# Recurrence operations of the two halves joined into one instruction each, router columns joined to the first up unit, two gated products given to VectorE

## The reference

```
q, k = l2norm(silu(h Wq)), l2norm(silu(h Wk));  v = silu(h Wv);  beta = sigmoid(h Wb)
u_t = beta_t * (v_t - S_{t-1}^T k_t)         # one state S (16 x 16) for each image and head
S_t = S_{t-1} + k_t u_t^T ;  o_t = S_t^T q_t # 256 tokens, one after the other
x1  = x + h + o Wo
n   = layernorm(x1);  p = softmax(n router_w), the two largest kept and normalised
y   = alpha * shared(n) + (1 - alpha) * sum_e p_e * ((silu(n Wg_e) * (n Wu_e)) Wd_e)
out = x1 + y ;  alpha = sigmoid(n sg_w + sg_b)
```

## Time and profile before

| | us |
|---|---|
| median of 3 runs (497.37 to 498.15) | 497.47 |
| the profiled execution | 497.98 |
| its span | 496.2 |
| VectorE busy in the span | 428.0 |
| TensorE busy | 425.9 |
| GpSimd busy | 414.0 |
| ScalarE busy | 349.7 |

### The profile page before, as it was taken

How to read it: one execution, slowest core, us unless ns; L and a number is a source line. 1 busy time by engine, 2 the same in 40 slices (tenths; PEclk the granted TensorE clock), 3 DMA queues, 4 the chain that set the end, 5 groups by cost and what they waited for, 6 DMA issues and landing times.

```text
span 496.2 us, 10722 instructions
## 1 busy us (share of the span) xinstructions
PE 425.9 (86%) x2464; PEld 391.3 (79%) x2464; DVE 428.0 (86%) x2546; ACT 349.7 (70%) x1039; POOL 414.0 (83%) x527
## 2 busy tenths in 40 slices
PE   0344276899999999999999999999999989899996
PEld 0233144789999989899898989898988979898996
DVE  2349989999999999999999999999999999997200
ACT  2795445686878787877778686878786848385763
POOL 5288699989899999999999898998999999896341
PEclk9855555999999999999999999999999999999999
DMA  7948373543323222323233332323222323200300
GB/s 203 223 100 159 94 180 100 111 103 111 79 68 88 72 78 74 92 65 102 68 84 87 81 89 78 89 72 83 80 83 74 83 78 86 81 28 0 114 2 16
DMA packets 44752, 44.12 MB, mean 89 GB/s; under 512 B 19920, under 2 KB 36496, under 8 KB 44688
## 3 DMA queue, kind: packets, MB, share of 16 engines
q1 hardware_dynamic: 40944, 40.87, 32.3%
q10 hardware_dynamic: 3744, 2.57, 1.8%
HBM read 37.13 MB, written 6.29 MB: 87 GB/s over the span
## 4 chain that ended last, share of the span: by engine, by line
DVE 73%; PE 11%; SPq 4%; issue 3%; POOL 3%; DMA 3%; ACT 2%; DVEq 0%; ACTq 0%; POOLq 0%
DVE Pr L1301 16%; DVE u L1303 15%; DVE bank L1305 15%; DVE SH L1309 12%; PE bank L427 2%; DMA k_scratch<-khl 2%; DVE st L1041 2%; SPq L249 2%; SPq L214 1%; DVE ss L1116 1%; PE bank L412 1%; DVE mv L1042 1%; DVE otok L1148 1%; DVE loT L1084 1%; PE bank L400 1%
## 5 line engine op out<-in xcount | busy, mean ns | idle before, releaser
L931 POOL TENSOR_TENSOR hid<-sg,ug 128x192 f32<-128x192 f32 x192 | 112.3, 608 | 23.0 <-ACT ug L669 21.4
L886 POOL TENSOR_TENSOR PQ<-SH,QB 128x768 f32<-128x768 f32 x62 | 112.5, 1835 | 5.8 <-DVE SH L1309 5.8
L1301 DVE TENSOR_TENSOR Pr<-SH,bank 128x96 f32<-128x96 f32 x512 | 104.8, 245 | 4.3 <-PE bank L361 3.9
L893 POOL TENSOR_TENSOR PQ<-PQ 128x768 f32<-128x768 f32 (+2 forms) x93 | 103.3, 1111 | 6.0
L1305 DVE TENSOR_TENSOR bank<-bank,u 128x96 f32<-128x96 f32 x512 | 106.5, 252 | 0.0
L427 PE MATMUL bank<-Wd,hidT 128*128 128x192 f32 x576 | 106.4, 326 | 0.0
L1303 DVE TENSOR_REDUCE u<-Pr 128x6 f32<-128x102 f32 x512 | 105.9, 247 | 0.0
L1309 DVE TENSOR_TENSOR SH<-SH,bank 128x96 f32<-128x96 f32 x512 | 103.0, 241 | 0.0
L427 PEld LDWEIGHTS bank<-Wd,hidT 128*128 128x128 f32 x576 | 95.3, 190 | 0.0
L668 ACT ACTIVATE sg<-bank 128x192 f32<-128x192 f32 x192 | 63.0, 328 | 45.0 <-PE bank L404 25.7
L361 PE MATMUL bank<-KR,Sel 128*128 128x384 f32 x128 | 58.3, 460 | 22.0 <-DVE SH L1309 12.5
(11 more groups left out here) (150 smaller groups left out, 836.6 us busy)
## 6 DMA issues: line engine op xcount, KB each, us to landing
QB<-q_scratch SPq DMA_DIRECT2D x64, 384.0 KB
k_scratch<-khl SPq DMA_DIRECT2D x64, 48.0 KB, 1.7
KR<-k_scratch SPq DMA_DIRECT2D x32, 96.0 KB, 2.4
q_scratch<-qn SPq DMA_DIRECT2D x64, 24.0 KB, 1.6
Wd<-in_L_ffn_w_down_dram SPq DMA_DIRECT2D x4, 288.0 KB, 8.0
out_dram<-xT SPq DMA_DIRECT2D x1, 896.0 KB, 5.2
Wlo_unsplit<-in_L_ffn_w_gate_dram ACTq DMA_DIRECT2D x1, 768.0 KB, 5.6
Wlo_unsplit<-in_L_ffn_w_up_dram ACTq DMA_DIRECT2D x1, 768.0 KB, 8.8
```

The source lines that it names most:

```text
L886: tt(PQ[:, at * BR * HP:(at + n) * BR * HP].rearrange("p (i b h) d -> p i b (h d)", i=n, b=BR), SH[:, lo:lo + n].rearrange("p i b h d -> p ...
L893: chained(tt(PQ[:, :, 0:w], PQ[:, :, 0:w], PQ[:, :, w:2 * w], ALU.add))
L931: tt(hid[:, r * H:(r + 1) * H], sg[:, m % RING], ug[:, m % RING], ALU.mult).then_inc(s_hid, 1)
L1301: v = each(lambda br: count(tt(Pr[:, br, i, :, 0:D], prev[:, br], KB[:, br], ALU.mult)), Sb)
```

## The change

- **Recurrence.** From chunk 1 on, `each` issues one instruction over both halves (192 elements, 204 in the reduction) instead of two. Each then waits for the end of the one before it. Chunk 0 keeps the halves.
- **Small VectorE work.** The statistics, which were two or three operations behind each other at one slot, are taken apart (`A_stats`, `A_mean`, `A_var`) and put at slots of their own; so are the parts of `A_low`. The operation that made 1 + rstd goes to ScalarE (`A_plus`).
- **Router.** Its 8 columns and the shared gate's column (twice, for an even width) stand before the first up unit's 384 columns, which makes that unit 394 wide; `Fa_logits` on TensorE and the copy h2T on ScalarE go. The logits are read from the first unit's bank.
- **Gated products.** Units 2 and 8 are multiplied by VectorE (`Fb_hidden`), straight from PSUM with the gate as scalar; ScalarE makes no `ug` for them and GpSimd has 10 products for each chunk instead of 12.
- **Orders.** The lists of all three engines are written anew. The rounded key copy `A_khi` moves from the end of one step to the start of the next on ScalarE.

```diff
+DVE_UNITS = (2, 8,)
+R = E + 2
+WHOLE = frozenset((0, 1, 2, 3, 4, 5, 6, 7, 8, 9, 10, 11, 12, 13, 14, 15, 16, 17, 18, 19, 20, 21, 22, 23, 24, 25, 26, 27, 28, 29, 30, 31, 32, 33, 34, 35, 36, 37, 38, 39, 40, 41, 42, 43, 44, 45, 46, 47, 48, 49, 50, 51, 52, 53, 54, 55, 56, 57, 58, 59, 60, 61, 62, 63))
...
-                        def each(fn, waits):
+                        def each(slot, fn, made):
+
                             got = []
-                            for br in range(BR):
-                                if waits[br] is not None:
-                                    dve.wait_ge(*waits[br])
-                                got.append(fn(br))
+                            for lo in range(BR) if c < 1 or slot not in WHOLE else (0,):
+                                hi = lo + 1 if c < 1 or slot not in WHOLE else BR
+                                for need in dict.fromkeys(made[lo:hi]):
+                                    if need is not None:
+                                        dve.wait_ge(*need)
+                                got += [fn(lo, hi)] * (hi - lo)
                             return got
-                        v = each(lambda br: count(tt(Pr[:, br, i, :, 0:D], prev[:, br], KB[:, br], ALU.mult)), Sb)
+                        v = each(slot, lambda lo, hi: count(tt(Pr[:, lo:hi, i, :, 0:D], prev[:, lo:hi], KB[:, lo:hi], ALU.mult)), Sb)
...
+            def Fb_hidden(q, p, m):
+
+                dve.wait_ge(s_ug, q * UN + (m + 1))
+                dve.wait_ge(s_gate, q + 1)
...
+                nc.vector.scalar_tensor_tensor(out=hid[:, r * H:(r + 1) * H], in0=unit_halves(m)[1],
+                                               scalar=gate[:, p, m:m + 1] if m < E else rden[:, p, 1:2],
+                                               in1=sg[:, m % RING], op0=ALU.mult, op1=ALU.mult).then_inc(s_hidv, 1)
...
-            def Fa_logits(f, p):
-                if f == 0:
-                    pe.wait_ge(s_wr, 80)
-                pe.wait_ge(s_h2T, f + 1)
-                pe.wait_ge(s_split, f + 1)
-                project(bFa[:, 0:E + 1], h2T[:, 0:P], h2T[0:C1, P:2 * P], Wr0[:, :], Wr1[:, :]).then_inc(s_lg, 1)
...
-                f(hiT[C1:P, p, P:2 * P], bFa[0:C1, P:2 * P], ACT.Copy)
-                f(h2T[:, 0:P], bFa[:, 0:P], ACT.Copy)
-                f(h2T[0:C1, P:2 * P], bFa[0:C1, P:2 * P], ACT.Copy).then_inc(s_h2T, 1)
+                f(hiT[C1:P, p, P:2 * P], bFa[0:C1, P:2 * P], ACT.Copy).then_inc(s_h2T, 1)
```

More of the change, by code:

```diff
@@ L48, in view, with columns @@
             return nc.alloc_sbuf_tensor_at(name + "_unsplit", place[name][1], F32, offset=place[name][0])
+        def columns(n):
+            return slice(0 if n == 0 else R + n * 2 * H, R + (n + 1) * 2 * H)
         def sem(name):
@@ L182, in later, with spare, hidden_made, unit_halves @@
             return n >= by
-        free = [b[:, i * 2 * H:(i + 1) * 2 * H] for b, n in (
-            (hid[:, :], 3), (sg[:, :, :].rearrange("p r h -> p (r h)"), 2), (ug[:, :, :].rearrange("p r h -> p (r h)"), 2),
-            (hidT[:, :, :, :].rearrange("p a k t -> p (a k t)"), 2)) for i in range(n)]
+        wide = R + 2 * H
+        free = [hid[:, 0:wide], hid[:, wide:wide + 2 * H], hid[:, wide + 2 * H:wide + 4 * H]] + [
+            b[:, i * 2 * H:(i + 1) * 2 * H] for b in (
+                sg[:, :, :].rearrange("p r h -> p (r h)"), ug[:, :, :].rearrange("p r h -> p (r h)"),
+                hidT[:, :, :, :].rearrange("p a k t -> p (a k t)")) for i in range(2)]
+        def spare(m):
+            return free[m % len(free)][:, 0:wide if m == 0 else 2 * H]
+        def hidden_made(f, m):
+            on_dve = sum(k <= m for k in DVE_UNITS)
+            return f * len(DVE_UNITS) + on_dve, f * (UN - len(DVE_UNITS)) + m + 1 - on_dve
+        def unit_halves(m):
+            at = R if m == 0 else 0
+            return bUp[m % 2][:, at:at + H], bUp[m % 2][:, at + H:at + 2 * H]
         def turn_half(g):
@@ L479, in step @@
                     at(1, fill, 0)
                     at(-1, Fb_up, 2)
-                    at(-2, Fb_down, 3)
-                    at(-2, Fb_turn, 4)
+                    at(3, A_h)
                     at(1, fill, 1)
[L484 to L512, removed]
@@ L658, in weights_hi1 @@
                     act.wait_ge(s_w1, m - len(free) + 1)
-                f(free[m % len(free)][C1:P].bitcast(F32R), raw1[C1:P, m], ACT.Copy).then_inc(s_whi, 1)
+                f(spare(m)[C1:P].bitcast(F32R), raw1[C1:P, columns(m)], ACT.Copy).then_inc(s_whi, 1)
             def unit(q, p, m):
@@ L767, in step @@
+                    once(c, 1, weights_hi1, 11)
+                    at(-1, Fa_h)
+                    at(3, A_plus)
+                    at(-2, unit, 9)
                     at(-1, Fa_hT)
@@ L772, in step @@
                     at(-1, Fa_exp)
+                    at(-2, hidden, 2)
                     table(c + 2, LN_EXP)
@@ L1313, in grow @@
                             return count(ins)
-                        Sb = state[:] = each(grow, v)
+                        Sb = state[:] = each(slot + 3, grow, v)
                         others(slot + 3)
```

430 lines of the change are left out of this document (256 added, 174 removed).

## The result

The changed kernel takes 521.1 us (519.05 to 521.49), the kernel before 497.8 on the same chip: ratio 1.046, 95% interval 1.044 to 1.048. It is slower, by 23 us. The forecast was 514.5 with a range of 505 to 523: the sign and the mechanism hold, the size was 6.6 us short. The profiled execution of the changed kernel took 521.49 us, its span 519.7, 23.5 more than before.

A forecast was written before the change was run, and what follows sets the result against it. VectorE was taken to bound the kernel. Terms +12.7 (eleven full chunks), +5.0 (chunks 13 to 15), +0.5 (chunk 1), +1.0 (head), -1.0 (tail) gave +18.2, cautiously 17: 515 profiled, 514.5 median; range 505 to 523.

The forecast's parts named there:

- What bounds: VectorE, from 59.71 to 450.81 us: a microsecond on it is one of the kernel; TensorE has 0.8 us room.
- The interval of a joined operation: In the recurrence, each start 0.035 us behind the previous end: 1.571 us a token instead of 1.32.
- New pair of keys: At each new key pair, a second wait on VectorE no longer hidden: 8 x 0.07 = 0.56 us a chunk.
- Small work: VectorE's small operations in each chunk show only beyond the free gaps: 1.6 to 1.7 us instead of 5.1.
- Chunks 13 to 15: The last chunks have little small work to hide: 80.5 us against 75.53, +5.0.
- Chunk 1: Its waits for others exceed a us; some go under the longer chunk: +0.5 us.
- Head: Before chunk 1, the key copy stands behind hhi and chunk 0's keys are on the chain: +1.0 us.
- Tail: Behind the recurrence, router matmuls go and TensorE enters with fewer transposes left: -1.0 us, bounds 0 and -2.5.
- Caution: Whole kernel: 17 us taken instead of +18.2, since pair cost and the extra 0.01 rest on few rows.
- Rival 1: In the recurrence, joined instructions pay, starting as soon as the engine is released: 485 us; 4%.
- Rival 2: In each chunk everything small hides and the pair costs nothing: 26.3 us a chunk, 497 to 505 us; 8%.
- Rival 3: A new wait for logits in the router chain stops VectorE 0.7 us in every chunk: 525 us; 12%.

The follow-up runs named there:

- the halves kernel: The changed kernel with every recurrence operation in two halves again, router, products and orders staying as changed: 503.9 us, ratio 1.012 to the kernel before.
- the fillers: 32 extra reductions of 8 elements a chunk on VectorE: 522.2 us in the changed kernel, 530.5 with its operations in halves; with adds instead, 664.4 and 668.4.
- the mixed kernel: The changed kernel with joined operations at only 17 of the 64 recurrence slots, halves elsewhere: 506.3 us, ratio 1.014 to the kernel before.

## Why the prediction was right, and where it was short

- **What bounds.** Right: a microsecond of VectorE is one of the kernel from chunk 1 to the end of chunk 15. TensorE's nearly full 25.2 of 26 did not matter; with 0.5 us taken from it the chunk stayed.
- **The interval of a joined operation.** Right: 0.388, 0.401, 0.401, 0.388 against 0.390, 0.398, 0.397, 0.386, a start 0.035 behind each end; 1.578 for a token in the rows shown (1.581 in medians over chunks 5 to 11), not 1.571. This made the sign, by halves against joined: 17.2 us. The 0.01 that is missing in a token makes 0.16 in the chunk's sixteen, the larger part of what the recurrence came out above the sum.
- **New pair of keys.** Right: 0.07 behind the end was predicted on top of the 0.035, 8 times. In medians over chunks 1 to 14 the first Pr of a pair starts 0.104 behind the end of SH at five of the eight places (0.069 more), 0.117 at one, and 0.133 at the two where the outputs' buffers are waited for too: 0.62 a chunk in place of 0.56. The trace's list of instructions shows of what it is made: a separate wait instruction of VectorE (line 1389, 0.021 us in the median) stands there, 128 times in the kernel. With the tokens: recurrence 25.9 a chunk (16 x 1.581 + 0.62), not 25.7.
- **Small work.** 27.51 - 25.9 = 1.6, as the sum had it, but the sum was badly added: its items (0.33, 0.28, twice 0.17, 0.28, 0.08, 0.05, 0.40) make 1.76, not 1.6 to 1.7. The items together were 0.15 too high and the slip hid it. The free gap (32 more operations for 0.03 us) and the products' 0.36 of 0.40 were each measured alone.
- **Chunks 13 to 15.** 27.43, 26.95 and 27.49 against 27.1, 26.7 and 26.7. Some 0.2 of each is the recurrence's, and 0.5 in the last is ScalarE's sg ahead of the product at 474.30; the rest was not followed.
- **Chunk 1.** 29.10. "Some go under the longer chunk" was wrong: 1.3 us for oT and 0.3 for the logits are 1.6, before's waits for oT and st were 1.5. A chunk of 27.5 with 1.6 on top is what came.
- **Head.** +1.35, expected +1.0, but the reason given is not shown: with the same orders ahead of it, chunk 1 started at 59.81 in halves and between 58.4 and 61.9 in the others. +1.35 is less than this spread, and +1.0 may be no more than luck. What sets this start stays open.
- **Tail.** -0.3, not -1.0. Neither of its two reasons, the router's matmuls and TensorE's lead at entry, was measured alone, so which of them gave too little stays open.
- **Caution.** I took 17 of a sum of 18.2 because two terms rested on few rows. Both stood.
- **Rival 1** (the joined pay): out by the halves kernel and by the fillers. So the rule of the Trainium skill, "VectorE: DVE Perf Modes", section "Rules for kernel authors", to minimise the count of operations, doesn't hold here: 960 fewer instructions than in halves, 17 us more. An independent operation starts before the one ahead has ended, by 0.08 us here; where two independent halves exist, that is worth more than the saved instructions. The Trainium skill, "VectorE: DVE Perf Modes", section "The DRAIN you can't avoid", makes this exception itself: a next operation that isn't held starts earlier. The prediction had left it out of rival 1.
- **Rival 2**: the pair costs more than nothing, and 1.6 of small work shows. **Rival 3**: VectorE waits for the logits 0.3 us in chunk 1 and 2.3 behind the recurrence, and in no chunk between; the slack held.

The 6.6 us: 2.1 in chunks 2 to 12, 1.35 in 13 to 15, 0.8 in chunk 1, 0.35 in the head, 0.7 in the tail, 1.2 for the caution; the rest is rounding. The largest term of the account, 2.1, is the 0.2 a chunk from tokens and pairs. No kernel tried here beats the one before.

## What to carry to other kernels

On a chain in which each operation needs the one before, count the distance from start to start in both forms before joining: two independent halves cost twice the fixed part, one whole costs the way from its end to the next start (here 0.33 against 0.39 to 0.40, so the split wins by a sixth, though it has twice the instructions). A joined operation gained here only where its gap got filled with work that would otherwise be paid, one operation to each gap, and lost where it stood empty; and mixing both forms cost at changes from halves to whole, in good part by a needless second wait. Count the waits ahead of a dependent start as well: a second one became an instruction of its own here and cost 0.07. Room on another engine is a property of the present period: what GpSimd could take at 27.5 us a chunk it could not at 26.1.

## What the runs showed of the hardware that I had not expected

- An addition of 8 elements with both inputs in SBUF took up to 1.81 us beside running GpSimd operations, 0.468 in the mean of 480; a reduction of as many elements with one input took the engine for 0.06. The recurrence's 192-wide operations with one input in PSUM, at 0.35, show nothing of it.
- From the same engine's end to a dependent start it is 0.035 us, at 64 elements as at 192. Where a separate wait instruction stands between them the start lies 0.104 behind the end: at a new pair of keys in the changed kernel, and in the mixed kernel where two counts of one counter are asked for.
- TensorE's granted clock was 0.52 and 0.65 in the 4 us behind a stop of 2.1 us in the halves kernel, and 1.00 again in 440 to 442.
